# The first recurrence of a two-layer AdaLN stack in a new order: state update inside the next chunk, mix ahead of the last levels, operands and norm on ScalarE, leaf blocks as tiles

## Chip, cores and metric

One core of one Trainium2 chip. The metric is the device time of one execution in microseconds (us), the median of the runs. In the profile the engines are PE (TensorE matmul), PEld (its weight loads), DVE (VectorE), ACT (ScalarE), POOL (GpSimd) and SP (which issues DMAs).

## What is computed

Two layers, each of a recurrence and a mixture of experts, on x of 2 batches x 1024 tokens x 128 channels. The change is in the recurrence of layer 0, which the reference writes as a scan over the tokens of each batch and head (2 heads of 64):

```
x_last = jnp.pad(x, ((0, 0), (1, 0), (0, 0)))[:, :t]
dxa = x_last - x
xm = x + dxa * miu_x
lora_h = jnp.tanh(xm @ A_lora).reshape(b, t, 5, -1)
miu = lambda_ + jnp.einsum('btfi,fic->fbtc', lora_h, B_lora)
w_in, k_in, v_in, r_in, g_in = x[None] + dxa[None] * miu
k = k_in @ Wk.T; v = v_in @ Wv.T; r = r_in @ Wr.T
g = jax.nn.silu(g_in @ Wg.T)
w = td_miu + jnp.tanh(w_in @ td_A) @ td_B
def step(S, inp):            # decay = exp(-exp(w))
    ri, ki, vi, di = inp
    kv = ki[:, None] * vi[None, :]
    y = ri @ (S + uh[:, None] * kv)
    S = di[:, None] * S + kv
    return (S, y)
```

After it come a norm of y per head, the product with g, the projection Wo, the gated addition to x, and the norm that feeds the experts of layer 0.

## The kernel before

The program is four blocks of instructions, one after the other: a setup, the recurrence of layer 0 (`rwkv_phase`, the only one that changes), the experts of layer 0, and layer 1. Within a block each engine has a queue written out by hand; an engine runs its queue strictly in order, and semaphores (`s_...`) tie the queues together. No scheduler reorders anything.

The recurrence goes over the sequence in 8 chunks of 128 tokens, both batches at once (N = 256 columns). `steps` calls `front` and then `step(i, q, prepare, tail)` for chunks 0 to 7: all have `prepare` but the last, all have `tail` but the first. What one step holds:

- **Levels** (`for m in lv`, 7 of them): the decays are multiplied up in a tree. On each level DVE writes `tot` (L595) and half of `rl` (L596), ACT copies the other half of `rl` and half of `kl` (L765, L767), POOL writes the rest of `kl` (L686). Each level waits for the one below on the other engines. PE takes scores of 32x32 leaf blocks from levels 0 to 4 (`leaf_scores`, L855) and wider ones from levels 5 and 6 (L913, L919); level 7 gives the operands for the state.
- **Attention and state**: DVE masks the leaf scores (`prod`, L613), adds up five partial blocks (`leafs`, L616) and copies them into the diagonal of `att` (L621); ACT copies the blocks off the diagonal (L784 to L786). PE transposes `kl[7]` (L929), ACT copies it to `ktm` (L776), PE computes the output y (L938, L941) and k^T v (L946), DVE masks that and updates `state` (L626, L630).
- **prepare, for chunk i+1**: DVE normalises x (L504), PE transposes it (L799), ACT modulates it (L713), POOL takes the difference to the token before (L641), DVE forms `xm` (L510), PE, ACT and PE do the low-rank product (L804, L805, L718, L720, L814, L817), DVE and POOL mix five inputs (L518, L646), PE projects them (`project`, L822 to L838), ACT takes them out (L728 to L742).
- **tail, of chunk i-1**: statistics of y on DVE (L535, L539), their deviation on POOL (`deviation`, L655, L657), `yn` (L544), a transpose, the gate and Wo, the addition to x, and `moe_input`, the norm for the experts (L558 to L572, its deviation on POOL at L673, L675).

`keep_busy(n)` (L868) is n matmuls on constants whose result nobody reads. A step with a tail has 5 of them at its start and 2 x 2 further on. What lets an engine into step i is `start`:

```
if not isinstance(i, int) or i:
    eng.wait_ge(s_state, i * 3)
eng.wait_ge(s_gT, i + 1)
```

So every engine begins a step when the state of the chunk before has been written (L630) and the last projection has been taken out by ACT (L742).

## Time and profile before

| | |
|---|---|
| median of 3 runs | 767.53 us (767.01 to 770.05) |
| the profiled execution's own time | 770.7 us |
| its span in the profile | 768.6 us |
| mean granted clock of TensorE | 0.931 of full speed |
| busy: PE, DVE, ACT, POOL | 664.5, 432.5, 290.5, 277.2 us |
| recurrence of layer 0 in the span | from 23 to about 202.5 us |

A row of the timeline gives the start (us from the span's start), the duration (us; for "x4" from the first start to the last end), the engine, the line, the operation with output<-input, and in brackets how long the engine sat idle before it and who released it. A matmul of the program in float32 shows as two instructions ("x32" for 16 matmuls). "PEclk" and the figure after the PEld column in a row of windows are the clock that TensorE was granted, as a share of 2.4 GHz: 1.00 is 2.4 GHz and 0.50 is 1.2 GHz.

### The profile page before, as it was taken

Reading aid. Unit: us, or ns where it says so; the run is one execution under the profiler, and the core shown is the slowest. Engines: PE = TensorE matmul, PEld = TensorE weight load, DVE = VectorE, ACT = ScalarE, POOL = GpSimd, SP = SyncE. Lnnn points to the kernel's source line nnn. Section 1 sums busy time; section 2 is a strip of 40 time slices with the busy share of each in tenths; the row PEclk is TensorE's granted clock in tenths of the full one; section 3 lists DMA queues with packets and bytes.
Section 4 is the critical chain, followed back from the end, with each engine's and each line's share of the span. In section 5 each row is a group of like instructions: output and inputs, shape, how many; then the busy total and the mean of one; then the engine's idle time right before and its main releaser. Section 6 shows DMA issues by size and latency. Waiting matters only on the chain.

```text
span 768.6 us, 26385 instructions
## 1 busy us (share of the span) xinstructions
PE 664.5 (86%) x10885; PEld 558.9 (73%) x10885; DVE 432.5 (56%) x1364; ACT 290.5 (38%) x964; POOL 277.2 (36%) x418
## 2 busy tenths in 40 slices
PE   4688888889721979699999999999999799999996
PEld 4356666657611968478888888888887599898996
DVE  4357888886250322265867776776767455344443
ACT  0154444442110422145555454454544235333321
POOL 1235555553234456100324233342423243222216
PEclk9769999989955989599999999999999899999999
DMA  6691000000214573200000000000040247575553
GB/s 176 215 275 27 3 1 3 3 2 2 110 42 152 165 236 119 58 3 4 3 10 12 11 11 14 11 11 14 7 144 10 80 149 253 182 246 197 186 211 90
DMA packets 45910, 66.31 MB, mean 86 GB/s; under 512 B 5584, under 2 KB 34736, under 8 KB 42848
## 3 DMA queue, kind: packets, MB, share of 16 engines
q1 hardware_dynamic: 42368, 57.55, 24.1%
q0 software_dynamic: 3424, 7.08, 2.6%
q8 instruction: 87, 1.43, 0.7%
q14 instruction: 31, 0.25, 0.1%
HBM read 49.92 MB, written 19.02 MB: 90 GB/s over the span
## 4 chain that ended last, share of the span: by engine, by line
PE 53%; DVE 2%; DMA 1%; issue 1%; another core or an unknown queue 1%; ACT 0%; SPq 0%; POOL 0%; DVEq 0%; POOLq 0%
PE bank L1720 6%; PE quad L1578 5%; PE quad L1702 5%; PE quad L1704 5%; PE bank L1603 4%; PE pair L1540 3%; PE bank L1627 3%; PE bank L1640 2%; PE quad L1584 2%; PE pair L1542 2%; PE pair L1541 2%; PE bank L1643 2%; PE bank L1630 2%; PE pair L1565 2%; DMA f_xg<-moe_slots 1%
## 5 line engine op out<-in xcount | busy, mean ns | idle before, releaser
L1978 DVE TENSOR_TENSOR h_masked<-quad,const 128x1536 f32<-128x1536 f32 (+2 forms) x66 | 112.5, 1704 | 55.1 <-PE quad L1584 45.5
L1814 ACT ACTIVATE f_sa<-quad 128x256 f32<-128x256 f32 (+1 forms) x115 | 40.2, 352 | 94.9 <-PE quad L1704 77.1
L2092 DVE TENSOR_TENSOR f_hid<-f_sa,quad 128x256 f32<-128x256 f32 (+1 forms) x115 | 43.0, 380 | 55.2 <-ACT f_sa L1814 54.8
L1702 PE MATMUL quad<-f_xT,f_w 128*128 128x256 f32 (+1 forms) x190 | 51.4, 353 | 3.6 <-DVE f_hid L2092 3.6
L1720 PE MATMUL bank<-f_w,f_hid 128*128 128x128 f32 x390 | 50.7, 277 | 1.1 <-DVE f_hid L2095 0.9
L1720 PEld LDWEIGHTS bank<-f_w,f_hid 128*128 128x128 f32 x390 | 47.8, 192 | 3.6 <-DVE f_hid L2095 2.8
L1704 PE MATMUL quad<-f_xT,f_w 128*128 128x256 f32 (+1 forms) x190 | 50.2, 346 | 0.0
L2201 POOL DMA_INDIRECT moe_slots<-g_pay,g_slot x28 | 28.7, 1023 | 58.3 <-DVE g_pay L1946 43.2
L1578 PE MATMUL quad<-h_qk 32*128 32x128 f32 x1024 | 47.1, 298 | 0.0
L868 PE MATMUL bank<-const 128*128 128x256 f32 x140 | 37.3, 406 | 7.8 <-PEq L202 7.8
L1603 PE MATMUL bank<-h_qk,h_state 32*32 32x128 f32 x1024 | 42.5, 274 | 0.0
L1578 PEld LDWEIGHTS quad<-h_qk 32*128 32x128 f32 x1024 | 34.8, 187 | 10.3 <-issue 8.4
L1791 ACT ACTIVATE h_gT<-bank 128x128 f32<-128x128 f32 x64 | 17.8, 278 | 64.9 <-PE bank L1630 64.9
L1103 POOL DMA_INDIRECT moe_out<-e_yg,e_token x32 | 30.9, 965 | 28.5 <-DVE e_yg L1203 22.2
L2167 POOL TENSOR_TENSOR h_added<-h_added,mod_row 128x128 f32<-128x128 f32 x16 | 7.3, 455 | 93.8 <-ACT h_added L1787 93.8
L2269 POOL DMA_INDIRECT moe_out<-f_y,f_token x31 | 30.3, 977 | 28.9 <-DVE f_y L2104 20.4
L686 POOL TENSOR_TENSOR kl<-kl,tot 128x128 f32<-128x128 f32 x56 | 25.2, 449 | 40.6 <-DVE state L630 20.8
L1765 ACT ACTIVATE h_qk<-pair 128x256 f32<-128x256 f32 x64 | 24.5, 383 | 36.8 <-PE pair L1542 36.8
L1702 PEld LDWEIGHTS quad<-f_xT,f_w 128*128 128x128 f32 x190 | 32.3, 195 | 6.7 <-DVE f_hid L2092 3.9
L1704 PEld LDWEIGHTS quad<-f_xT,f_w 128*128 128x128 f32 x190 | 34.2, 195 | 3.4
L868 PEld LDWEIGHTS bank<-const 128*128 128x128 f32 x140 | 26.6, 203 | 11.4 <-issue 8.0
L1795 ACT ACTIVATE h_oT<-bank 128x128 f32<-128x128 f32 x64 | 17.8, 278 | 40.7 <-PE bank L1652 32.2
(380 smaller groups left out, 1840.0 us busy)
## 6 DMA issues: line engine op xcount, KB each, us to landing
f_w<-moe_w SPq DMA_DIRECT2D x23, 1088.0 KB, 5.2
e_w<-in_experts_dram SPq DMA_DIRECT2D x32, 257.5 KB
moe_slots<-blank SPq DMA_DIRECT2D x2, 2112.0 KB, 16.6
moe_slots<-zero SPq DMA_DIRECT2D x4, 516.0 KB, 4.0
e_xg<-moe_slots SPq DMA_DIRECT2D x8, 258.0 KB
f_xg<-moe_slots SPq DMA_DIRECT2D x12, 132.0 KB, 4.5
moe_w<-in_moe_w_dram SPq DMA_DIRECT2D x1, 1408.0 KB, 7.5
moe_w<-in_moe_w_dram SPq DMA_DIRECT2D x1, 1280.0 KB, 10.5
```

The costliest lines, as they stand in the source:

```text
L868: pe.matmul(bank[of][:, 0:N], cst("ident"), const[:, 0:N], start=True, stop=True)
L1103: pool.indirect_dma_start(out=t["moe0_out"], out_offset=bass.IndirectOffsetOnAxis(ap=token_of[s][:, k:k + 1], axis=0), in_=yg[s][:, k, :], ...
L1578: last = pe.matmul(quad[:, h, a * P:(a + 1) * P], qk[q][head(h), 1 - a, :], qk[q][head(h), a, :], start=True, stop=True, tile_position=(h ...
L1603: pe.matmul(left[head(h), part * P:(part + 1) * P], states[k][head(h), (0 if part else 2 * D):(D if part else 3 * D)], qk[k][head(h), 1 - ...
L1702: pe.matmul(up_bank(n, f)[:, 0:s], w[:, F1 + TAIL1 + f * P:F1 + TAIL1 + (f + 1) * P], x_of(n)[:, 0:s], start=True, stop=True)
L1704: pe.matmul(up_bank(n, f)[:, T1:T1 + s], w[:, f * P:(f + 1) * P], x_of(n)[:, 0:s], start=True, stop=True).then_inc(f_up, 1)
L1720: pe.matmul(acc[k], hid[n % 2][:, f, cols], w[:, 2 * F1 + f * C:2 * F1 + (f + 1) * C], start=(f == 0), stop=False)
L1814: act.activation(sa[g % 3][:, 0:s], up_bank(n, f)[:, 0:s], ACT.Silu).then_inc(f_sa, 1)
L1978: dve.tensor_tensor(masked[k % 4][:, :, a * P:z * P], quad[:, :, a * P:z * P], cst("causal")[:, None, a * P:z * P].to_broadcast([P, HPG, ( ...
L2092: dve.tensor_tensor(hid[n % 2][:, f, 0:s], sa[g % 3][:, 0:s], up_bank(n, f)[:, T1:T1 + s], ALU.mult)\
L2201: pool.indirect_dma_start(out=t["moe1_slots"], out_offset=bass.IndirectOffsetOnAxis(ap=slot[:, b * 2 + k:b * 2 + k + 1], axis=0), in_=pay[ ...
L2269: pool.indirect_dma_start(out=t["moe1_out"], out_offset=bass.IndirectOffsetOnAxis(ap=token_of[n % 2][:, k:k + 1], axis=0), in_=yg[n % 2][: ...
```

## The change

- `start` no longer waits for the state but for the last score matmul of the chunk before (`s_leafmm`). The state update is now `carry`, on DVE in the next step behind its level 2, behind the norm's statistics.
- Masked leaf scores are no longer reduced and copied into `att`. One addition folds five partial blocks into three (`s_sum`), and PE multiplies each 32x32 block with `v` by itself, as a tile on the array's diagonal: 24 small matmuls for each batch.
- `rd` and `kd` (operands of the leaf scores with the bonus) and the centring of x come from ACT instead of DVE. ACT's bias column `nbias` is made once. `rd`, `kd` and `gT` are doubled.
- DVE's `mix` moves from behind the last level to behind level 4, POOL's to behind level 5. `gate` moves to the step's start, `normalise` behind `mix`, `output` to the step's end. The norm for the experts is split and runs two chunks behind instead of one.
- On PE, `lora` comes one level earlier, `mix` ahead of level 4's scores, the projections ahead of the scores of levels 5 and 6, the transpose of x(i+2) at the end of step i. The transposes of `kl[7]` and the product with `ktm` stand behind the output matmuls. ACT copies `ktm` as the last thing of a step. Of 9 `keep_busy` matmuls in a middle step 2 are left.

The diff, cut to its core:

```diff
-            if not isinstance(i, int) or i:
-                eng.wait_ge(s_state, i * 3)
+            if i:
+                eng.wait_ge(s_leafmm, i)
             eng.wait_ge(s_gT, i + 1)
...
+            def carry(n, q):
+
+                dve.tensor_tensor(kv[:, :, :], bank[5][:, N:2 * N].rearrange("p (b n) -> p b n", b=BATCH),
+                                  cst("head2")[:, None, :].to_broadcast([P, BATCH, P]), ALU.mult).then_inc(s_state, 1)
+                dve.wait_ge(s_state, n * 3 + 1)
+                for b in range(BATCH):
+                    dve.scalar_tensor_tensor(out=state[:, b, :], in0=state[:, b, :], scalar=tots[q][LEVELS][:, b:b + 1],
+                                             in1=kv[:, b, :], op0=ALU.mult, op1=ALU.add).then_inc(s_state, 1)
...
-                    norm(i + 1)
-                if tail:
-                    statistics(i - 1, 1 - q)
-
-                rh, kh = halves(rl[0], 0), halves(kl[0], 0)
-                dve.tensor_scalar(halves(rd, 0)[:, :, 0], rh[:, :, 0], bonus[:, 0:1], None, ALU.mult).then_inc(s_diag, 1)
-                dve.tensor_copy(halves(rd, 0)[:, :, 1], rh[:, :, 1]).then_inc(s_diag, 1)
-                dve.tensor_copy(halves(kd, 0)[:, :, 0], kh[:, :, 0]).then_inc(s_diag, 1)
-                dve.tensor_scalar(halves(kd, 0)[:, :, 1], kh[:, :, 1], bonus[:, 0:1], None, ALU.mult).then_inc(s_diag, 1)
+                    last_column(i + 1)
+                gate(i, q)
...
+                    if i and m == LEVELS - 1:
+                        dve.wait_ge(s_kv, i)
...
-                    if tail and m == 0:
-                        normalise(i - 1, 1 - q)
                     if prepare and m == 1:
                         lora_input(i + 1)
+                    if m == 2:
+                        if i >= 2:
+                            moe_statistics(i - 2)
+                        if tail:
+                            statistics(i - 1, 1 - q)
+                            carry(i - 1, 1 - q)
                     if m == 4:
+                        if prepare:
+                            mix(i + 1)
+                        if i >= 2:
+                            moe_scale(i - 2)
                         if tail:
-                            dve.wait_ge(s_zg, i)
-                        gate(i)
-                        if tail:
-                            output(i - 1, 1 - q)
-                if prepare:
-                    mix(i + 1)
+                            normalise(i - 1, 1 - q)
...
-                                  ALU.add).then_inc(s_leaf, 1)
-                dve.wait_ge(s_leaf, i + 1)
-                for k in range(4):
-                    rows = slice(k * LEAF, (k + 1) * LEAF)
-                    dve.tensor_copy(att[rows, :, rows], leafs[rows, :, :]).then_inc(s_att, 1)
+                dve.tensor_tensor(prod[:, :, 0:2 * LEAF], prod[:, :, 0:2 * LEAF], prod[:, :, 2 * LEAF:4 * LEAF],
+                                  ALU.add).then_inc(s_sum, 1)
                 if tail:
...
-                    if prepare and m == 1:
+                    if prepare and m == 0:
                         difference(i + 1)
-                    if tail and m == 0:
-                        deviation(i - 1, 1 - q)
-                    if tail and m == 2:
-                        gated_heads(i - 1, 1 - q)
+                    if m == 2:
+                        if i >= 2:
+                            moe_deviation(i - 2, q)
+                        if tail:
+                            deviation(i - 1, 1 - q)
+                    if prepare and m == 5:
+                        mix(i + 1)
                 if tail:
+                    gated_heads(i - 1, 1 - q)
...

+            def centre(n):
+                for b in range(BATCH):
+                    c = n + b * CHUNKS
+                    act.activation(xn[:, b, :], x_bc[:, b, n, :], ACT.Identity, bias=nbias[:, c:c + 1],
+                                   scale=rstd[:, c:c + 1]).then_inc(s_xn, 1)
...
+                kd, k0 = halves(kds[q], 0), bank[2][:, 0:N].rearrange("p (k h e) -> p k h e", h=2, e=1)
+                act.activation(kd[:, :, 0], k0[:, :, 0], ACT.Copy).then_inc(s_evac, 1)
+                act.activation(kd[:, :, 1], k0[:, :, 1], ACT.Copy, scale=bonus[:, 0:1]).then_inc(s_evac, 1)
...
+                rd, r0 = halves(rds[q], 0), bank[3][:, 0:N].rearrange("p (k h e) -> p k h e", h=2, e=1)
+                act.activation(rd[:, :, 0], r0[:, :, 0], ACT.Copy, scale=bonus[:, 0:1]).then_inc(s_diag, 1)
+                act.activation(rd[:, :, 1], r0[:, :, 1], ACT.Copy).then_inc(s_diag, 1)
...
                                    ACT.Copy).then_inc(s_rc, 1)
                     if prepare and m == 0:
                         modulate(i + 1)
-                    if tail and m == 1:
-                        scale_heads(i - 1, 1 - q)
-                    if prepare and m == 3:
+                    if prepare and m == 2:
                         lora_tanh(i + 1)
-                act.wait_ge(s_ktT, i + 1)
-                act.activation(ktm[:, :, :], bank[4][:, 0:N].rearrange("p (b n) -> p b n", b=BATCH),
-                               ACT.Copy).then_inc(s_ktm, 1)
+                    if m == 3 and i + 2 < CHUNKS:
+                        centre(i + 2)
+                    if m == 5:
+                        if i:
+                            act.wait_ge(s_kv, i)
+                        if prepare:
+                            decay_tanh(i + 1)
+                            take_k_v(i + 1, 1 - q)
+                        if tail:
+                            scale_heads(i - 1, 1 - q)
                 if prepare:
-                    decay_tanh(i + 1)
-                    take_k_v(i + 1, 1 - q)
+                    take_decay_r_g(i + 1, 1 - q)
...
-                    take_decay_r_g(i + 1, 1 - q)
+                    act.wait_ge(s_ktT, i + 1)
+                    act.activation(ktm[:, :, :], bank[4][:, 0:N].rearrange("p (b n) -> p b n", b=BATCH),
+                                   ACT.Copy).then_inc(s_ktm, 1)
...
-                keep_busy(5 if tail else 2)
+                keep_busy(2)
...
-                    if tail and m == 1:
-                        keep_busy(2)
-                        transpose_heads(i - 1, 1 - q)
-                    if prepare and m == 2:
-                        lora(i + 1)
-                    elif m == 2:
-                        keep_busy(3, 2)
-                    if tail and m == 3:
-                        output(i - 1, 1 - q)
+                    if m == 1:
+                        if prepare:
+                            lora(i + 1)
+                        else:
+                            keep_busy(3, 2)
+                    if m == 3:
+                        if prepare:
+                            mix(i + 1)
+                        else:
+                            keep_busy(3, 2)
                 if prepare:
-                    mix(i + 1)
+                    project_k_v(i + 1)
+                if tail:
+                    transpose_heads(i - 1, 1 - q)
+                if prepare:
+                    project_decay_r_g(i + 1)
+                else:
+                    keep_busy(5, 2)
...
                 pe.wait_ge(s_r, i * LEVELS + 7)
                 pe.wait_ge(s_rc, i * 2 * LEVELS + 14)
-                if tail:
-                    pe.wait_ge(s_gated, i)
-                for b in range(BATCH):
-                    last = pe.transpose(bank[4][:, b * P:(b + 1) * P], kl[7][:, b * P:(b + 1) * P], cst("ident"))
-                last.then_inc(s_ktT, 1)
-                if prepare:
-                    project(i + 1)
-                else:
-                    keep_busy(5, 2)
-                pe.wait_ge(s_att, i * 4 + 4)
-                pe.wait_ge(s_off, i * 3 + 3)
+                if i:
+                    pe.wait_ge(s_state, i * 3)
+                pe.wait_ge(s_sum, i + 1)
                 for b in range(BATCH):
                     pe.matmul(bank[5][:, b * P:(b + 1) * P], rl[7][:, b * P:(b + 1) * P], state[:, b, :],
                               start=True, stop=False, skip_group_check=True)
+                    for l in (0, 1, 4):
+                        for h in range(RW_HEADS):
+                            for k in range(4):
+                                rows = slice(k * LEAF, (k + 1) * LEAF)
+                                pe.matmul(bank[5][rows, b * P + h * RW_DIM:b * P + (h + 1) * RW_DIM],
+                                          prod[rows, h * BATCH + b, l * LEAF:(l + 1) * LEAF],
+                                          v_sb[rows, b, h * RW_DIM:(h + 1) * RW_DIM], start=False, stop=False,
+                                          tile_position=(k * LEAF, k * LEAF), skip_group_check=True)
+                    if b == 0:
+                        pe.wait_ge(s_off, i * 3 + 3)
                     for h in range(RW_HEADS):
-                        pe.matmul(bank[5][:, b * P + h * RW_DIM:b * P + (h + 1) * RW_DIM], att[:, h * BATCH + b, :],
-                                  v_sb[:, b, h * RW_DIM:(h + 1) * RW_DIM], start=False, stop=True,
-                                  skip_group_check=True)
-                pe.wait_ge(s_ktm, i + 1)
-                for b in range(BATCH):
-                    last = pe.matmul(bank[5][:, N + b * P:N + (b + 1) * P], ktm[:, b, :], v_sb[:, b, :], start=True,
-                                     stop=True, skip_group_check=True)
+                        last = pe.matmul(bank[5][:, b * P + h * RW_DIM:b * P + (h + 1) * RW_DIM],
+                                         att[:, h * BATCH + b, :], v_sb[:, b, h * RW_DIM:(h + 1) * RW_DIM],
+                                         start=False, stop=True, skip_group_check=True)
+                if prepare:
+                    pe.wait_ge(s_k, i * LEVELS + 7)
+                    if tail:
+                        pe.wait_ge(s_gated, i)
+                    for b in range(BATCH):
+                        last = pe.transpose(bank[4][:, b * P:(b + 1) * P], kl[7][:, b * P:(b + 1) * P], cst("ident"))
+                    last.then_inc(s_ktT, 1)
+                    pe.wait_ge(s_ktm, i + 1)
+                    for b in range(BATCH):
+                        last = pe.matmul(bank[5][:, N + b * P:N + (b + 1) * P], ktm[:, b, :], v_sb[:, b, :], start=True,
+                                         stop=True, skip_group_check=True)
```

**ACT, end of a middle step.** Names: `ktm` the transposed keys, `tw` to `eg` the projections of the next chunk, `att` the score blocks, `rl<-rl_1` the first level of the next step. Before:

```order
L767 ACTIVATE kl<-kl 128x2x64
L776 ACTIVATE ktm<-bank 128x256
L724 ACTIVATE tw<-quad 64x256
L728 ACTIVATE kl_1<-quad 128x256
L729 ACTIVATE v_sb<-quad 128x256
L784 ACTIVATE att<-pair 64x4x64
L785 ACTIVATE att<-pair 32x4x32
L786 ACTIVATE att<-pair 32x4x32
L735 ACTIVATE ew<-quad,td_miu 128x256
L737 ACTIVATE tot_1<-ew 128x256
L742 ACTIVATE eg<-quad 128x256
L765 ACTIVATE rl<-rl_1 128x128
```

After the change:

```order
L782 ACTIVATE zT<-bank,beta,gamma 128x256
L796 ACTIVATE rl<-rl 128x2x64
L798 ACTIVATE kl<-kl 128x2x64
L758 ACTIVATE ew<-quad,td_miu 128x256
L760 ACTIVATE tot_1<-ew 128x256
L765 ACTIVATE rd<-quad,bonus 128x128
L766 ACTIVATE rd<-quad 128x128
L768 ACTIVATE eg<-quad 128x256
L819 ACTIVATE att<-pair 64x4x64
L821 ACTIVATE att<-pair 32x4x32
L824 ACTIVATE ktm<-bank 128x256
L796 ACTIVATE rl<-rl_1 128x128
```

The copy of `ktm` moved from the head of this stretch to its very end, right ahead of the next step's first level.

**PE, from the last leaf scores of a middle step to the next step.** Names: `lh` and `xx` the low-rank and mixed inputs, `pair` the scores, `bank<-const` both the transposes (128x128) and `keep_busy` (128x256). Before:

```order
L855 MATMUL pair<-rl,kl 32x32 x16
L814 MATMUL quad<-lh,b_pad 128x256 x4
L817 MATMUL quad<-lh,b_last 128x256
L913 MATMUL pair<-rl,kl 32x32 x8
L919 MATMUL pair<-rl,kl 64x64 x4
L929 MATMUL bank<-const,kl 128x128 x2
L822 MATMUL quad<-xx,td_a 64x256
L838 MATMUL quad<-xx,wT 128x256
L938 MATMUL bank<-state,rl 128x128
L941 MATMUL bank<-v_sb,att 128x64 x2
L946 MATMUL bank<-v_sb,ktm 128x128 x2
L868 MATMUL bank<-const 128x256 x5
```

After the change:

```order
L879 MATMUL quad<-xx,wT 128x256
L959 MATMUL pair<-rl,kl 32x32 x8
L965 MATMUL pair<-rl,kl 64x64 x4
L916 MATMUL bank<-wT,zT 128x128 x2
L838 MATMUL quad<-const,xn 128x128 x2
L979 MATMUL bank<-state,rl 128x128
L985 MATMUL bank<-v_sb,prod 32x64 x24
L992 MATMUL bank<-v_sb,att 128x64 x2
L985 MATMUL bank<-v_sb,prod 32x64 x24
L1000 MATMUL bank<-const,kl 128x128 x2
L1004 MATMUL bank<-v_sb,ktm 128x128 x2
L911 MATMUL bank<-const 128x256 x2
```

The transposes of `kl` moved from ahead of the projections to behind all output matmuls; 48 block matmuls joined them there.

**DVE, the middle of a step after the change.** Names: `xm` the input of the low-rank product, `nst` and `h_pay` the norm for the experts, `gst` and `gmv` the norm of y.

```order
L509 SCALAR_TENSOR_TENSOR xm<-dxa,miu,hT 128x256
L601 TENSOR_TENSOR tot<-tot 128x32
L602 TENSOR_TENSOR rl<-rl,tot 128x32x4
L567 BN_STATS nst<-x_sb 128x6 x2
L571 BN_AGGR nmv<-nst 128x2 x2
L574 SCALAR_TENSOR_TENSOR h_pay<-x_sb,nmv,sbw 128x128 x2
L535 BN_STATS gst<-bank 128x6 x4
L539 BN_AGGR gmv<-gst 128x2 x4
L556 TENSOR_TENSOR kv<-bank,const 128x256
L560 SCALAR_TENSOR_TENSOR state<-state,tot,kv 128x128 x2
L601 TENSOR_TENSOR tot<-tot 128x16
L602 TENSOR_TENSOR rl<-rl,tot 128x16x8
```

Six groups of the tail that stood at a step's end or start now stand between levels 2 and 3.

## Rows read from the trace of the kernel before

**Rows 1.** The page: the granted clock in 40 slices of the span.

```profile
PEclk9769999989955989599999999999999899999999
```

**Rows 2.** Windows: PE, PEld, DVE, ACT, POOL busy, clock, DMA share, GB/s.

```profile
98.00:117.00 19.00, 16.04 (x257) 11.23 (x256) 15.97 (x60) 9.20 (x31) 10.96 (x20) 1.00 0.00 1
```

**Rows 3.** State updates (one tile) in four windows: durations in ns, first and last start.

```profile
L630 DVE SCALAR_TENSOR_TENSOR state<-state,tot,kv x2: 347/350/352, 96.9 to 97.1; 128x128 f32<-128x128 f32 x2
...
L630 DVE SCALAR_TENSOR_TENSOR state<-state,tot,kv x2: 347/350/352, 115.6 to 115.9; 128x128 f32<-128x128 f32 x2
...
L630 DVE SCALAR_TENSOR_TENSOR state<-state,tot,kv x2: 345/348/352, 153.7 to 154.0; 128x128 f32<-128x128 f32 x2
L630 DVE SCALAR_TENSOR_TENSOR state<-state,tot,kv x2: 347/350/353, 175.1 to 175.3; 128x128 f32<-128x128 f32 x2
```

**Rows 4.** Timeline of DVE, one step (chunk 3).

```profile
98.34 0.61 DVE L535 BATCH_NORM_STATS2 gst<-bank 128x6 f32<-128x64 f32 x4
99.05 0.38 DVE L539 BATCH_NORM_AGGREGATE gmv<-gst 128x2 f32<-128x6 f32 x4
...
102.75 0.67 DVE L510 SCALAR_TENSOR_TENSOR xm<-dxa,miu,hT 128x256 f32<-128x256 f32 x1
...
109.37 0.81 DVE L613 TENSOR_TENSOR prod<-pair,const 128x640 f32<-128x640 f32 x1
...
112.50 0.49 DVE L558 BATCH_NORM_STATS2 nst<-x_sb 128x6 f32<-128x128 f32 x2
...
113.38 0.62 DVE L565 SCALAR_TENSOR_TENSOR h_pay<-x_sb,nmv,sbw 128x128 f32<-128x128 f32 x2
```

**Rows 5.** Timeline of POOL, the same step.

```profile
100.19 1.17 POOL L657 TENSOR_TENSOR grs<-grs,eps_pow 128x4 f32<-128x4 f32 x1
...
101.76 0.61 POOL L641 TENSOR_TENSOR dxa<-hT 128x256 f32<-128x256 f32 x1
...
104.36 1.09 POOL L686 TENSOR_TENSOR kl<-kl,tot 128x128 f32<-128x128 f32 x2
...
108.03 3.01 POOL L646 TENSOR_TENSOR xx<-xx,hT 128x256 f32<-128x256 f32 x5
```

**Rows 6.** Timeline of ACT, the same step.

```profile
99.01 0.81 ACT L713 ACTIVATE hT<-quad,mod_col 128x128 f32<-128x128 f32 x2 [0.97 <-PE quad L799]
...
108.11 0.39 ACT L776 ACTIVATE ktm<-bank 128x256 f32<-128x256 f32 x1 [0.77 <-PE bank L929]
```

**Rows 7.** Timeline of PE, the same step.

```profile
106.99 0.33 PE L913 MATMUL pair<-rl,kl 64*32 64x32 f32 x16
107.25 0.45 PE L919 MATMUL pair<-rl,kl 64*64 64x64 f32 x8
107.63 0.44 PE L929 MATMUL bank<-const,kl 128*128 128x128 f32 x2
...
109.90 0.70 PE L826 MATMUL quad<-xx,wT 128*128 128x256 f32 x2 [0.54 <-POOL xx L646]
...
112.59 0.46 PE L938 MATMUL bank<-state,rl 128*128 128x128 f32 x2
...
113.95 0.66 PE L946 MATMUL bank<-v_sb,ktm 128*128 128x128 f32 x4
```

**Rows 8.** Timeline of PE, layer 1: tiles of 32x32 on the diagonal (L1603).

```profile
343.38 0.31 PE L1603 MATMUL bank<-h_qk,h_state 32*32 32x128 f32 x4
...
343.51 0.29 PE L1603 MATMUL bank<-h_qk,h_state 32*32 32x128 f32 x4
```

**Rows 9.** Windows, PE alone: PE busy, clock, in the step of chunk 6.

```profile
166.00:167.00 1.00, 0.46 (x2) 1.00 0.05 16
167.00:168.00 1.00, 1.00 (x5) 0.55 0.00 0
```

**Rows 10.** Timeline, the stage's edges: ACT's first level of chunk 0, DVE's last norm.

```profile
40.06 0.32 ACT L765 ACTIVATE rl<-rl 128x128 f32<-128x128 f32 x1
...
201.88 0.61 DVE L572 SCALAR_TENSOR_TENSOR h_pay<-h_pay,nrstd,sbw 128x128 f32<-128x128 f32 x2 [0.66 <-POOL nrstd L675]
```

More of the change, by code:

```diff
@@ L519, in mix, with gate @@
                                              op0=ALU.add, op1=ALU.mult).then_inc(s_scaled, 1)
-            def gate(n):
-                dve.scalar_tensor_tensor(out=gT[:, :], in0=eg[:, :], scalar=1.0, in1=bank[0][:, N:2 * N], op0=ALU.add,
+            def gate(n, q):
+                dve.scalar_tensor_tensor(out=gTs[q][:, :], in0=eg[:, :], scalar=1.0, in1=bank[0][:, N:2 * N], op0=ALU.add,
                                          op1=ALU.mult).then_inc(s_gate, 1)
             def front():
-                norm(0)
+                last_column(0)
                 lora_input(0)
@@ L615, in step, with last_norms @@
                 dve.wait_ge(s_prod, i + 1)
[L616 to L633 removed]
+                dve.tensor_tensor(prod[:, :, 0:2 * LEAF], prod[:, :, 0:2 * LEAF], prod[:, :, 2 * LEAF:4 * LEAF],
+                                  ALU.add).then_inc(s_sum, 1)
+                if tail:
+                    output(i - 1, 1 - q)
+            def last_norms(n, q):
+                moe_statistics(n - 1)
+                normalise(n, q)
+                moe_scale(n - 1)
+                output(n, q)
+                moe_statistics(n)
+                moe_scale(n)
+            steps(dve, front, step, (statistics, last_norms))
         @block.gpsimd
@@ L922, in step @@
                 last.then_inc(s_leafmm, 1)
-                pe.wait_ge(s_k, i * LEVELS + 7)
+                if tail:
+                    output(i - 1, 1 - q)
+                if i + 2 < CHUNKS:
+                    transpose_x(i + 2)
                 pe.wait_ge(s_r, i * LEVELS + 7)
                 pe.wait_ge(s_rc, i * 2 * LEVELS + 14)
-                if tail:
-                    pe.wait_ge(s_gated, i)
-                for b in range(BATCH):
-                    last = pe.transpose(bank[4][:, b * P:(b + 1) * P], kl[7][:, b * P:(b + 1) * P], cst("ident"))
-                last.then_inc(s_ktT, 1)
-                if prepare:
-                    project(i + 1)
-                else:
-                    keep_busy(5, 2)
-                pe.wait_ge(s_att, i * 4 + 4)
-                pe.wait_ge(s_off, i * 3 + 3)
+                if i:
+                    pe.wait_ge(s_state, i * 3)
+                pe.wait_ge(s_sum, i + 1)
                 for b in range(BATCH):
```

81 lines of the change are left out of this document (43 added, 38 removed).

## The prediction

> **What bounds the kernel now.** I read the granted clock on the page first [rows 1], then the windows by stage, then the state updates, then the timeline of each engine in one step. The recurrence fills 23 to 202.5 us of a span of 768.6, and nothing else changes. A middle step takes 18.8 us from state to state (96.9 to 115.6 [rows 3]). In 19 us DVE is busy 15.97, the most of any engine but PE, whose 16.04 hold nine `keep_busy` matmuls [rows 2]. The reader should see in DVE's timeline an engine that hardly rests and does one thing after another that all others wait for: levels, mix, leaf sums, expert norm, state [rows 4]. So DVE's queue is the bound, and the state at its end is what all engines' `start` waits for.
>
> The second thing to see is the clock. In the step of chunk 6 PE worked 0.46 of a microsecond and then was granted 0.55, that is the fall from 2.4 to 1.2 GHz [rows 9]. Ahead of that fall PE had only small tiles and waited for POOL's mix. That step took 21.4 us from state to state (153.7 to 175.1) where its neighbours take 18.8 [rows 3]: one low stretch costs **2.6 us**.
>
> **What the change takes from DVE.** Per step it removes the sum and the copies of the leaf blocks (the time between the mask's end at 110.18 and 112.50, 2.3 us [rows 4]), the centring of x and four operand copies (an estimate of 1.4 from the two-to-four-instruction groups beside them), and adds one fold of 256 columns. I put the fold at 0.4, an estimate between the 0.67 of `xm` with its 256 columns and half the 0.81 of the mask with 640 [rows 4]. Net about 3.3 us less DVE work in a step. If DVE stayed the bound, that would be the gain.
>
> **But the queue of ACT closes a new loop.** ACT now copies `ktm` as a step's last thing, and its first level of the next step stands right behind. The copy waits for PE's transposes of `kl[7]`, which wait behind all output matmuls, which wait for the fold of the leaf scores. I follow this loop for a middle step at 2.4 GHz, from ACT's first level at 0:
>
> 1. ACT: two level copies (0.45, an estimate from the 0.32 of one [rows 10]), then the modulation, 0.81 [rows 6]: 1.3. It cannot run earlier, though DVE and POOL have their halves done.
> 2. POOL's difference 0.61 [rows 5]: 1.9. DVE's `xm` 0.6 [rows 4]: 2.5. DVE's level 2, 0.3: 2.8.
> 3. DVE: first part of the expert norm, 112.50 to 114.00 in the rows of before, 1.5: 4.3. Statistics of y, 98.34 to 99.43, 1.1 [rows 4]: 5.4. `carry` follows on DVE (1.1), off this path.
> 4. POOL: deviation, from the statistics at 99.43 to 101.36 [rows 4, 5], 1.9: 7.3. In its queue the levels 3, 4 and 5 stand behind it: 1.09 for two [rows 5], so 1.4 up to its mix: 8.7. DVE's mix is ready by then (levels 3 and 4 done at about 7.1, first output 0.4 later) and so is PE's low-rank part (about 6).
> 5. POOL's mix: three of five, 3.01 x 3/5 = 1.8 [rows 5]: 10.5, and 0.1 to PE.
> 6. PE: from the first projection at 109.90 to the output matmuls at 112.59, 2.7 [rows 7], plus the transpose of the heads that now stands in between, 0.3: 13.6. Scores of levels 5 and 6, 106.99 to 107.70, 0.7 [rows 7]: 14.3.
> 7. DVE: mask 0.86, fold 0.4 [rows 4]: 15.6. PE's product with Wo and its transpose of x fit in here, as do ACT's `rd`, `eg` and `att` copies: ACT is free of them at about 16.3.
> 8. PE: output matmuls 1.36 (112.59 to 113.95 [rows 7]) plus the 48 blocks. They are 96 instructions. Tiles of 64x32 with 32 columns came every 16 ns (16 from 106.99 to 107.25 [rows 7]); tiles of 32x32 on the diagonal with 128 columns every 32 ns (four from 343.38 to 343.51 [rows 8]). The blocks have 64 columns; I take 16 ns, 1.5 us, because they hold half the columns of the diagonal tiles, and keep 0 (hidden by overlap) and 32 ns (3.1) as ends: 18.5.
> 9. Transposes of `kl` 0.44 [rows 7], ACT's `ktm` 0.39 [rows 6]: **19.3**.
>
> So the loop is 0.5 us longer than DVE's 18.8. What DVE gives up turns into waiting.
>
> The Trainium skill, "TensorEngine Tiling (Array Packing)", section "Key Properties", says that a change of tiling mode drains TensorE. This would add to item 8, where a step now changes mode four times more; at the 0.27 that I estimate for one matmul's passage it would make the sum 1.1 larger per step, 20.4. No row here separates such a drain.
>
> **The edges.** Chunk 0 has neither item 3 nor the heads: about 16.8. Chunk 1 has no expert norm yet: 17.8. Chunks 2 to 6 take 19.3 each, 96.5. The last chunk and what follows it: levels 2, norms, levels and fold to 11.5, output 14.4, statistics, two expert norms and the drain to about 25.0, against the 26.8 up to 202.5 [rows 10], since the sum and the copies are gone. Together 156.1 against 162.4 [rows 10]: **-6.3 us** at full clock.
>
> **The clock.** Before, PE waited 0.54 us ahead of its second projection [rows 7] and had `keep_busy` in the longer gaps. Now seven of nine are gone, and by the items above PE has only small tiles and a 32-row mix from 3.9 to 5.9, then 0.4 us of tiles, a half-microsecond matmul near 9.4, and starts its projections at 10.6. That is emptier than the stretch ahead of the fall in chunk 6 [rows 9], and it comes in every step with `prepare`. After the fall come the projections, scores and heads (item 6), which are now on the loop. I charge the 2.6 of rows 3, a little less since part of the low stretch lies under waits: 2.5 for each of seven steps, +17.5. Ends: 0 if the clock holds, and 3.4 a step (all of items 6, at twice the time).
>
> The Trainium skill, "TensorE: Matmul & The Clock Gate", section "What's actually happening", has the same rule against this change: "the default state is throttled, and activity releases the throttle". By that rule the sum has this term, without it it is 761; the trace agrees as far as the fall of rows 9 goes.
>
> **Sum.** -6.3 + 17.5 = +11.2. The profiled execution took 770.7 in all (768.6 span and 2.1 around), so it would be 781.9; it stands 3.2 over the median of the runs, which gives 778.7 there. I forecast **778 us**.
>
> **Rivals.**
> - *The clock holds.* The leaf tiles and 48 new blocks count as enough work. For it: before, the clock stood through PE's waits for POOL, such as 0.54 us [rows 7], in all middle steps but one [rows 1]. Against it: the step where it didn't. Then only the -6.3 is left: **761 us, faster**. It decides from fewer than about two and a half low stretches (6.3 / 2.5).
> - *DVE remains the bound.* ACT's wait for `ktm` is covered, because DVE and POOL start earlier than I think and the modulation is not what they wait for. Then a step is 18.8 - 3.3 = 15.5, seven of them -23: **745 us**. Against it is ACT's queue, where `ktm` stands ahead of the first level with nothing between.
> - *The clock falls in half of the steps*, or for half as long: +8.75 - 6.3: **770 us**.
> - *The blocks are slow*, 32 ns an instruction, or drain the array: +1.5 in seven steps, 10.5 more: **789 us**.
>
> **How the numbers follow.** About 0.5% (3.8 us) is what a measurement of this kernel can tell from no change, so the middle band is 763.7 to 771.4. Forecast (771 to 787 by itself) 0.45, of it 0.43 slower and 0.02 in the band. Clock holds 0.25, of it 0.20 faster and 0.05 in the band. DVE bound 0.09, faster. Half 0.11: 0.01, 0.07, 0.03. Slow blocks 0.10, slower. Sums: faster 0.30, same 0.14, slower 0.56. The range runs from 757 to 790: left out are the DVE rival, the top half of the slow blocks and the lowest part of the held clock, 0.18 together. It takes in the unknown price of the blocks and of the fold.
>
> **What would show it.** Right: granted clock of 0.50 in a part of each step; DVE idle before level 1, waiting for ACT; ACT idle before `ktm`, waiting for PE; POOL's levels 3 waiting for DVE's statistics; steps of 21 to 22 us, or 19.3 where the clock holds. The blocks should take 0.8 us per batch. Wrong: a clock of 1.00 throughout, or steps under 18 us with ACT's first level hard behind `eg`. Then the tail of PE, or the gap before the projections, is shorter than I made it.

## The result, and the profile after

| | before | after |
|---|---|---|
| median of runs (range) | 768.76 us (767.01 to 770.05, 4 runs) | **793.79 us** (790.75 to 796.16, 4 runs) |
| profiled execution / span | 770.7 / 768.6 us | 790.75 / 789.0 us |
| mean granted clock | 0.931 | 0.902 |
| recurrence, ACT's first level to DVE's last norm, us from the span's start | 40.06 to 202.5 | 40.3 to 224.4 |

The change makes the kernel slower: ratio 1.0325, 95% interval 1.0273 to 1.0377. Forecast were 778 us, in a range of 757 to 790; the sign is right, the size is not. Here and below a median is that of all runs of a set, while a ratio and its interval compare the fast runs of both kernels alone.

All of it is in the recurrence: it grew by 21.6 us, from 162.4 to 184.1, and the rest of the profiled execution took 1.6 less. The page of the kernel after: part 1, the line of the granted clock in 40 slices (19.7 us each), and from part 5 the row of DVE's level product:

```profile
PE 675.9 (86%) x11555; PEld 566.1 (72%) x11555; DVE 410.7 (52%) x1282; ACT 300.4 (38%) x1011; POOL 276.0 (35%) x418
...
PEclk9687886895895598879999999999999999999999
...
L601 DVE TENSOR_TENSOR tot<-tot 128x128 f32<-128x128 f32 (+6 forms) x56 | 17.0, 303 | 32.2 <-ACT kl L798 30.5
```

Two things are to be seen. The clock, in slices 3 to 11, was near 1.00 before but for single dips [rows 1]; now nearly every slice of the stage is below. And DVE idles 32.2 us ahead of the level line `tot`, 30.5 of it for ACT's level, where DVE's wait for that was 4.8 us before: the engine that was the bound now waits for ACT's level.

One step from ACT's first level to the next, with the part of it at 1.2 GHz in brackets, of chunk 0 to 6, then the last to the end of the stage:

```
before  19.8 (11.0) 18.8 (0)    18.9 (0)   18.8 (0)    18.8 (0)    19.2 (0)   21.4 (6.8)  26.8
after   18.8 (4.2)  22.3 (10.2) 21.6 (6.8) 25.8 (16.0) 22.2 (11.3) 21.0 (3.4) 25.8 (16.7) 26.6 (3.7)
```

17.8 us of the stage were at 1.2 GHz before, 72.4 after. The loop that the forecast followed stands in the timeline of the step of chunk 3, each engine by itself (start and duration in us, then idle time before it and who ended it). ACT:

```profile
128.50 0.38 ACT L824 ACTIVATE ktm<-bank 128x256 f32<-128x256 f32 x1 [6.47 <-PE bank L1000]
128.78 0.31 ACT L796 ACTIVATE rl<-rl 128x128 f32<-128x128 f32 x1
```

DVE:

```profile
120.34 0.82 DVE L622 TENSOR_TENSOR prod<-pair,const 128x640 f32<-128x640 f32 x1 [5.21 <-PE pair L965]
...
129.42 0.23 DVE L601 TENSOR_TENSOR tot<-tot 128x64 f32<-128x64 f32 x1 [5.98 <-ACT kl L798]
...
130.71 0.67 DVE L509 SCALAR_TENSOR_TENSOR xm<-dxa,miu,hT 128x256 f32<-128x256 f32 x1 [0.86 <-POOL dxa L646]
```

POOL:

```profile
130.06 0.61 POOL L646 TENSOR_TENSOR dxa<-hT 128x256 f32<-128x256 f32 x1 [6.77 <-ACT hT L733]
```

ACT idles 6.47 us for PE's transposes of `kl`, copies `ktm`, and only then takes the level. DVE and POOL stand still for six microseconds each behind that. PE in the same step:

```profile
110.61 0.39 PE L898 MATMUL pair<-rl,kl 64*32 64x32 f32 x32 [1.71 <-POOL kl L693]
112.32 0.72 PE L861 MATMUL quad<-xx,td_a 128*64 128x256 f32 x2 [1.32 <-POOL xx L651]
113.66 1.22 PE L865 MATMUL quad<-xx,wT 128*128 128x256 f32 x2 [0.62 <-POOL xx L651]
...
122.47 1.50 PE L985 MATMUL bank<-v_sb,prod 32*32 32x64 f32 x48
```

Windows of the same step (us; PE, PEld, DVE, ACT, POOL busy; granted clock; DMA share; GB/s):

```profile
111.00:112.00 1.00, 0.00 (x1) 0.00 (x0) 1.00 (x4) 0.61 (x3) 0.79 (x3) 1.00 0.00 0
112.00:113.00 1.00, 0.68 (x2) 0.19 (x2) 1.00 (x3) 0.00 (x0) 1.00 (x3) 0.88 0.00 0
113.00:114.00 1.00, 0.38 (x2) 0.35 (x2) 1.00 (x5) 0.38 (x1) 1.00 (x2) 0.50 0.00 0
114.00:124.00 10.00, 10.00 (x95) 7.15 (x94) 4.10 (x12) 4.69 (x16) 3.36 (x6) 0.50 0.01 2
124.00:133.00 9.00, 8.53 (x133) 6.75 (x134) 2.58 (x11) 2.41 (x9) 1.65 (x4) 0.50 0.01 2
133.00:134.00 1.00, 1.00 (x4) 0.33 (x3) 0.90 (x7) 0.00 (x0) 0.85 (x2) 0.88 0.00 0
```

PE stands almost still at 111, as the forecast had it, and the clock falls from 1.00 to 0.50 within the next two. What was not in the forecast: it stays at 0.50 for 20.5 us (112.8 to 133.2) although PE was busy for 10.00 of 10.00 from 114 on. The projections, scores, output matmuls and transposes, all of the loop's PE part, ran at half speed.

### The profile page after: what moved, and what is told of

It is laid out like the page before. It is cut to its first block, busy times and chain, and to the rows that moved or that the text cites. A ratio compares the mean times of both kernels' runs of the same rounds, so it can differ in the third digit from the quotient of the medians.

```text
span 789.0 us, 27723 instructions
## 1 busy us (share of the span) xinstructions
PE 675.9 (86%) x11555; PEld 566.1 (72%) x11555; DVE 410.7 (52%) x1282; ACT 300.4 (38%) x1011; POOL 276.0 (35%) x418
## 4 chain that ended last, share of the span: by engine, by line
PE 51%; DVE 2%; DMA 1%; issue 1%; another core or an unknown queue 1%; ACT 0%; POOL 0%; SPq 0%; DVEq 0%; POOLq 0%
PE bank L1778 6%; PE quad L1636 5%; PE quad L1760 5%; PE quad L1762 4%; PE bank L1661 4%; PE pair L1598 3%; PE bank L1685 3%; PE bank L1698 2%; PE quad L1642 2%; PE pair L1599 2%; PE pair L1600 2%; PE bank L1688 2%; PE bank L1701 2%; PE pair L1623 2%; DMA f_xg<-moe_slots 1%
## 5 line engine op out<-in xcount | busy, mean ns | idle before, releaser
L1849 ACT ACTIVATE h_gT<-bank 128x128 f32<-128x128 f32 x64 | 17.8, 278 | 64.3 <-PE bank L1688 64.3
L1853 ACT ACTIVATE h_oT<-bank 128x128 f32<-128x128 f32 x64 | 17.8, 278 | 42.4 <-PE bank L1710 32.9
L601 DVE TENSOR_TENSOR tot<-tot 128x128 f32<-128x128 f32 (+6 forms) x56 | 17.0, 303 | 32.2 <-ACT kl L798 30.5
L1598 PE MATMUL pair<-h_hT,hla_wq 128*128 128x128 f32 x128 | 30.7, 323 | 2.5 <-POOL h_hT L2219 1.8
```

The source lines that it names most:

```text
L1598: pe.matmul(proj[:, 0:P], W["q"][:, cols], hT[b][:, :], start=True, stop=True)
```

## The experiments

Three questions are open after this. How much is the clock, how much the order? Is it the loop through `ktm`? And what do the 32x32 blocks cost? Ratios are to the kernel before, which ran with each set: median 767.19 us beside e1 to e4, 765.04 beside e5 to e8. A filler (`keep_busy(1)`) is one matmul, in two instructions of 0.26 us each. The stage is counted from ACT's first level to DVE's last norm in the profiled execution; what comes behind it took 561 to 570 us in these executions, so steps and stages are compared first. The columns on the stage and its steps are each from one profiled execution.

| | median us | ratio to before | stage us | of it at 1.2 GHz | later steps us |
|---|---|---|---|---|---|
| before | 767.19 / 765.04 | | 162.4 | 17.8 | 18.8 |
| after | 793.79 | 1.0325 | 184.1 | 72.4 | 21.0 to 25.8 |
| e1_fill | 775.17 | 1.0122 | 168.1 | 6.8 | 19.9 |
| e2_before_two | 801.51 | 1.0458 | 192.1 | 119.5 | 23.9 |
| e3_early | 758.78 | 0.9883 | 155.0 | 33.5 | 16.9 to 17.2 |
| e4_early_fill | 760.89 | 0.9941 | 154.0 | 0.6 | 18.2 |
| e5_start9 | 797.20 | 1.0413 | 187.4 | 44.4 | 21.1 or 23.3 |
| e6_fill_oneblock | 766.05 | 0.9987 | 159.8 | 7.3 | 19.0 |
| e7_early_light | 753.39 | 0.9837 | 145.1 | 0.6 | 16.9 to 17.1 |
| e8_early_re | 750.24 | 0.9820 | 146.1 | 10.6 | 16.8 to 17.0 |

### e1_fill: filler matmuls in the two gaps

```diff
                         if prepare:
                             mix(i + 1)
+                            keep_busy(4)
 ...
                 if prepare:
+                    keep_busy(3)
                     project_k_v(i + 1)
```

> The changed kernel with seven of the removed constant matmuls put back, but at places where PE waits for POOL: four ahead of level 4's scores and three behind them, in every step that prepares. Nothing else moves. Theory (the clock): the stretches at 1.2 GHz in the recurrence shrink from 72 us to under 15, and of the 28 us that they cost by the changed kernel's trace at least 20 come back: 765 to 773 us. Rival 1 (the clock is granted low for another reason, such as the small tiles): low time unchanged, 792 to 798. Rival 2 (the loop through ACT is itself much longer than 19.3 us a step): clock at 1.00 and still 778 or more.

Measured: 775.17 us (768.41 to 779.47), ratio 1.0122 (1.0077 to 1.0167). 6.8 us at 1.2 GHz instead of 72.4; the page's clock line reads

```profile
PEclk9789999999855889799999999999999899999999
```

The steps are 22.7, 19.4, and then 19.9 five times, all at full clock from the second on. So the clock is more than half of the loss (1.0325 to 1.0122), and even without it a middle step is 1.1 us longer than before. The low time came out as the theory had it; the time is 2 us above its range, since 18.6 us came back where it asked for 20. Rival 2's 778 is not reached, but a part of what it says is there: a middle step is 0.6 longer than the 19.3 forecast. The fillers themselves cost in the first two steps: in chunk 1 k's projection begins 10.15 us after the first level, in the kernel after 9.15. In the middle steps they cost nothing, and there the loop can be checked item by item. The step of chunk 3 begins with ACT's level at 99.81. POOL:

```profile
108.45 3.28 POOL L651 TENSOR_TENSOR xx<-xx,hT 128x256 f32<-128x256 f32 x5
```

PE:

```profile
110.47 0.70 PE L865 MATMUL quad<-xx,wT 128*128 128x256 f32 x2 [0.43 <-POOL xx L651]
...
114.09 0.71 PE L916 MATMUL bank<-wT,zT 128*128 128x128 f32 x4
...
115.63 0.46 PE L981 MATMUL bank<-state,rl 128*128 128x128 f32 x2 [0.62 <-DVE prod L625]
116.02 0.87 PE L987 MATMUL bank<-v_sb,prod 32*32 32x64 f32 x48
116.83 0.66 PE L994 MATMUL bank<-v_sb,att 128*128 128x64 f32 x4
117.32 0.44 PE L981 MATMUL bank<-state,rl 128*128 128x128 f32 x2
...
118.99 0.39 PE L1002 MATMUL bank<-const,kl 128*128 128x128 f32 x2
```

ACT:

```profile
119.41 0.38 ACT L824 ACTIVATE ktm<-bank 128x256 f32<-128x256 f32 x1 [3.37 <-PE bank L1002]
119.69 0.31 ACT L796 ACTIVATE rl<-rl 128x128 f32<-128x128 f32 x1
```

| loop item, us after ACT's first level | forecast | e1_fill |
|---|---|---|
| POOL's mix begins | 8.7 | 8.64 |
| k's projection begins | 10.6 | 10.66 |
| scores end (the next matmul begins) | 14.3 | 14.28 |
| output matmuls begin, after mask and fold | 15.6 | 15.82 |
| transposes of `kl` begin | 18.5 | 19.18 |
| ACT's next first level | 19.3 | 19.88 |

The chain was traced rightly through four engines to within 0.2 us; the largest part of the rest is the output matmuls, 3.36 us (115.63 to 118.99) instead of 2.86. The fillers did not hold this step back: k's projection still waited 0.43 for POOL.

### e3_early: `ktm` before the output matmuls

This undoes one part of the change, the place of the transposes, and leaves its clock alone. They go to another PSUM bank, since the old one is in use there.

```diff
                 last.then_inc(s_leafmm, 1)
+                if prepare:
+                    pe.wait_ge(s_k, i * LEVELS + 7)
+                    pe.wait_ge(s_rc, i * 2 * LEVELS + 14)
+                    for b in range(BATCH):
+                        last = pe.transpose(bank[2][:, b * P:(b + 1) * P], kl[7][:, b * P:(b + 1) * P],
+                                            cst("ident"))
+                    last.then_inc(s_ktT, 1)
                 if tail:
                     output(i - 1, 1 - q)
 ...
-                    for b in range(BATCH):
-                        last = pe.transpose(bank[4][:, b * P:(b + 1) * P], kl[7][:, b * P:(b + 1) * P], cst("ident"))
-                    last.then_inc(s_ktT, 1)
```

and ACT's copy of `ktm` goes ahead of its three `att` copies.

> The changed kernel with the transposes of kl[7] right behind the last score matmuls (into the free half of another PSUM bank) and ACT's copy of them ahead of its att copies, so that ACT no longer waits for the output matmuls before the next step's first level. No constant matmuls added. Theory (the loop closes through ACT's ktm): about 2.7 us a step at full clock and up to 6 where the clock is low, 7 steps: 766 to 776. Rival (DVE or PE is right behind, or the clock falls for longer since the gaps stay): 783 to 792.

Measured: **758.78 us** (752.72 to 777.61), ratio 0.9883 (0.9836 to 0.9929), better than expected. The ten runs spread wide, with mean granted clocks from 0.936 down to 0.895 (e1's and e4's lowest is 0.934), so this median is the least steady of the table. In the profiled execution, a step at full clock takes 16.9 to 17.2 us instead of 19.9, and the time at 1.2 GHz is 33.5 us. The releaser of the waits shows that the loop is gone. PE and ACT of e3, chunk 6, each from its own timeline:

```profile
164.29 0.44 PE L973 MATMUL quad<-const,kl 128*128 128x128 f32 x2
...
165.84 0.46 PE L986 MATMUL bank<-state,rl 128*128 128x128 f32 x2 [0.66 <-DVE prod L625]
```

```profile
164.77 0.38 ACT L819 ACTIVATE ktm<-quad 128x256 f32<-128x256 f32 x1
...
165.82 0.27 ACT L825 ACTIVATE att<-pair 32x128 f32<-32x128 f32 x1
```

The copy waits for nothing, and ACT is free at 166.09 while PE is only beginning its output matmuls. They now lie beside the next step's levels. The place of two pieces of work, the transposes and ACT's copy, decides the sign of the whole change.

### e4_early_fill: both

> Both edits together: early ktm and the seven constant matmuls in PE's gaps. Theory (clock and loop are separate terms): 747 to 757, faster than both kernels. Rival (the fillers now delay PE, which starts the next step late because output matmuls and k^T v run into it): 760 to 770.

Measured: 760.89 us (758.0 to 766.09), ratio 0.9941 (0.9901 to 0.9981). The two do not add: the rival's range held, not the theory's. The clock is almost clean (0.6 us low), but the steps are 18.2 instead of 17.1. PE of e4, just before k's projection:

```profile
158.16 1.56 PE L911 MATMUL bank<-const 128*128 128x256 f32 x6
159.66 0.65 PE L861 MATMUL quad<-xx,td_a 128*64 128x256 f32 x2
160.23 0.70 PE L865 MATMUL quad<-xx,wT 128*128 128x256 f32 x2
```

Neither projection has a wait ahead of it; in e3 the first waits 1.00 and k's 0.55 for POOL. The fillers are in front, and PE is late by them. A filler is free only inside a gap, and with `ktm` early the gap is shorter than seven of them.

### e2_before_two: the kernel before with two fillers a step

The other side of the same question: if fillers matter this much, how much do the seven that the change drops matter to the old order?

```diff
-                keep_busy(5 if tail else 2)
+                keep_busy(2)
                 start(pe, i)
 ...
-                if tail:
-                    keep_busy(2)
 ...
                     if tail and m == 1:
-                        keep_busy(2)
                         transpose_heads(i - 1, 1 - q)
```

> The kernel before with the constant matmuls of a middle step cut from nine to two, nothing else changed. Theory (the clock): low stretches appear in most steps; at 2.6 us for one of 6.8 us that is 5 to 13 us more, 773 to 781. Rival (in the kernel before PE is not on the path that ends a step, since DVE is busy throughout, so a low clock is mostly hidden): within 3 us of before, 766 to 771.

Measured: 801.51 us (799.47 to 801.62), ratio 1.0458 (1.0383 to 1.0534), much more than either theory said. Every step from chunk 1 to 6 has 17.1 us at 1.2 GHz and takes 23.9 instead of 18.8. DVE of this kernel in one step, two of the waits that it did not have before:

```profile
142.74 2.05 DVE L518 SCALAR_TENSOR_TENSOR xx<-quad,lamb,dxa 128x256 f32<-128x256 f32 x5 [1.19 <-PE quad L817]
...
153.18 0.42 DVE L626 TENSOR_TENSOR kv<-bank,const 128x256 f32<-128x256 f32 x1 [2.58 <-PE bank L943]
```

At half speed PE takes DVE's place as the bound. Seven dummy matmuls, 3.6 us of PE's time a step, are worth 34 us (801.51 - 767.19) to the kernel.

### e5_start9: nine fillers, all at the step's start

```diff
-                keep_busy(2)
+                keep_busy(9 if tail else 2)
                 start(pe, i)
```

> The changed kernel with the same seven constant matmuls put back, but all at the step's start, where PE has work anyway, instead of in its waits for POOL. Theory (what counts is the empty stretch between the low-rank part and the projections): the clock still falls in most steps, low time in the recurrence stays above 35 us, 785 us or more, and the start is delayed by 1.5 us a step. Rival (the sum of work per step is what counts): low time as in the kernel with fillers in the gaps, 775 to 780.

Measured: 797.2 us (794.66 to 806.94), ratio 1.0413 (1.035 to 1.0476). A middle step has as many fillers as in e1, and the time is no better than with two. Of the 44.4 us at 1.2 GHz 20.5 lie in chunk 0, which has no more fillers here than in the kernel after (its low time was 4.2 us there, in another execution). In chunks 1 to 6, which have nine, it is 23.8 us, against 64.4 with two and 0 in e1. So the number helps the clock too, but only the gaps ahead of the projections kept it up throughout. And at the start they cost time: a step at full clock takes 21.1 us instead of 19.9, since the leaf tiles and PE's low-rank product stand behind them (L843 begins 5.4 us after ACT's first level, in e1 2.7).

### e6_fill_oneblock: what the blocks cost

e1 with 16 instead of 48 block matmuls in a step, 64 instructions fewer; part of the attention within 32 tokens is left out.

```diff
-                    for l in (0, 1, 4):
+                    for l in (0,):
```

> The kernel with seven fillers in the gaps, and of the three blocks per head and row group only the first multiplied with v: 16 block matmuls instead of 48, so part of the attention within 32 tokens is left out of the output. Theory (the blocks stand on the loop at 17 ns an instruction): 64 instructions fewer, 1.1 us a step, steps of 18.8 instead of 19.9 at full clock, 8 us less in all. Rival (hidden behind ACT's copies): no change. Rival 2 (less work brings the clock down): low stretches come back.

Measured: 766.05 us (760.21 to 768.41), ratio 0.9987 (0.9945 to 1.0029). The steps take 19.0 instead of 19.9: 0.9 us for 64 instructions, 14 ns each. PE's output matmuls in chunk 3 of e6:

```profile
114.69 0.46 PE L981 MATMUL bank<-state,rl 128*128 128x128 f32 x2 [0.61 <-DVE prod L625]
115.08 0.43 PE L987 MATMUL bank<-v_sb,prod 32*32 32x64 f32 x16
...
117.15 0.39 PE L1002 MATMUL bank<-const,kl 128*128 128x128 f32 x2
```

They take 2.46 us (114.69 to 117.15) where e1's take 3.36: the same 0.9. So the blocks are on the loop at full price (nothing hides them), and that price is near the 16 ns taken; the slow-blocks rival is out. All 96 are 1.3 us of a step by these 14 ns.

### e7_early_light and e8_early_re: the version that beats both

e7 is e3 with two fillers behind the mix (`keep_busy(2)` after `mix(i + 1)`); e8 has three there and none at the start, and moves the expert norm out of the way of the statistics of y:

```diff
                     if m == 2:
-                        if i >= 2:
-                            moe_statistics(i - 2)
                         if tail:
                             statistics(i - 1, 1 - q)
-                            carry(i - 1, 1 - q)
+                        if i >= 2:
+                            moe_statistics(i - 2)
                     if m == 4:
                         if prepare:
                             mix(i + 1)
-                        if i >= 2:
-                            moe_scale(i - 2)
                         if tail:
+                            carry(i - 1, 1 - q)
                             normalise(i - 1, 1 - q)
+                if i >= 2:
+                    moe_scale(i - 2)
```

and on POOL `moe_deviation` goes behind the last level.

> Early ktm with only two constant matmuls added, between the mix and level 4's scores. Theory: they fit in PE's wait for POOL, so a step keeps the 17.1 us that the early version shows at full clock, and the low time in the recurrence falls from 33 us to below 14: 7 to 10 us less than the early version, 748 to 753. Rival (two are too few): as the early version, 755 to 760.

> Early ktm, three constant matmuls after the mix and none at the step's start; DVE takes the statistics of y ahead of the expert norm's first part and the state update behind its mix, and the expert norm's deviation moves behind POOL's last level. Theory: the deviation of y is out of POOL's way 1.4 us earlier, PE reaches its low-rank part 0.5 us earlier, so a middle step takes 16.2 to 16.7: 742 to 748. Rival (PE's low-rank part is right behind and sets the mix): 16.8 to 17.1 a step, 748 to 753.

Measured: e7 753.39 us (750.84 to 754.56), ratio 0.9837 (0.9792 to 0.9881), 17.1 a step and 0.6 us low: as the theory had it, at the upper end of its range. Two fillers in the first of PE's gaps were enough in its profiled execution. e8 **750.24 us** (749.37 to 755.08), ratio 0.982 (0.9769 to 0.9871), 16.7 to 17.0 a step and 10.6 low, all of it in chunk 0: its theory (16.2 to 16.7 a step, 742 to 748 us) missed, its rival's figures came out. Between the two the intervals overlap, and the stage of e8 is no shorter than e7's; that its reordering gained is shown only by the middle step, 0.1 to 0.3 us. The gain on before is settled for both: 16 to 17 us of the stage. One step of e8 in the windows:

```profile
107.50:124.40 16.90, 15.07 (x342) 10.82 (x341) 14.70 (x50) 10.65 (x37) 10.63 (x20) 1.00 0.01 3
```

DVE is busy 14.70 of 16.90, so DVE is near to being the bound again, as the rival "DVE remains the bound" wanted, though not at its 15.5 us; most of the change's saving on DVE then shows as time.

## Why the prediction was wrong in size and right in sign

**DVE's load fell as said, and became waiting.** DVE's busy time on the page went from 432.5 to 410.7 us, 2.7 for each of eight chunks, where 3.3 was said. The waits in the profile after and e3 show that at full clock the saving was lost to the loop.

**The loop through `ktm` was real.** e1 confirms items 1 to 7 to 0.2 us, and e3, which moves the transposes and their copy and nothing else of the computation, takes 2.8 us off each step at full clock.

**Item 8 was mis-sized: it put the changes between whole array and tiles at nothing.** It had 2.86 for the output matmuls, 1.36 of them for those of before and 1.5 for the blocks; they took 3.36. Over the 1.36 they took 2.00 more with 96 block instructions (e1) and 1.10 more with 32 (e6). That is 14 ns an instruction, 1.34 for all 96 and a little under the 1.5 put, and 0.65 that does not grow with the number of blocks. The row of the blocks in e1 agrees with the 14: 0.87 us for 48, less the 0.21 of a single one, are 0.66 for 47 distances. The 0.65 stands over the four changes between whole array and tiles in a step, 0.16 each, if each costs the same. Part of it can be seen in the starts. PE of the kernel before, behind the 112.59 of [rows 7]:

```profile
112.88 0.56 PE L941 MATMUL bank<-v_sb,att 128*128 128x64 f32 x4
113.28 0.44 PE L938 MATMUL bank<-state,rl 128*128 128x128 f32 x2
```

From the state product to what follows it were 0.29 us there (112.59 to 112.88), and 0.39 in e1 where blocks follow; `att` took 0.40 up to the next product, and 0.49 in e1 where blocks stand ahead. The Trainium skill, "TensorEngine Tiling (Array Packing)", section "Key Properties", has a rule that a change of tiling mode drains TensorE. A fixed price at each change agrees with it in sign, though no run separates a drain from other causes, such as the first weight loads; the prediction's estimate beside its sum, 1.1 a step, was 1.7 times the 0.65.

**The edges were a little short as well.** Chunk 0: 18.8 less the price of its 4.2 us at 1.2 GHz (0.30 for each, see below), an estimated 17.5 where 16.8 was put. Chunk 1: e1's 19.4 less the 1.0 by which its fillers delayed k's projection, 18.4 where 17.8 was put. The last chunk takes 26.6 (e1, all at full clock), 25.0 was put. Of the 5.9 us in all some 4 are the half microsecond of output matmuls, eight times. The stage at full clock comes to 17.5 + 18.4 + 5 x 19.9 + 26.6 = 162.0 us, not 156.1: the gain of 6.3 is nearly gone, **0.4** in its place. With the clock held the changed kernel would take about 769 in the profiled execution (790.75 - 22.1), where before took 770.7: hardly any gain, so the rival "the clock holds, 761" would have missed too.

**The clock term was right in kind and low in size.** 184.1 - 162.0 = 22.1 us against 17.5. What failed in this term is the length of a low stretch: it was charged at the price of the 6.8 us of chunk 6 in each of seven steps, 48 us in all, and there were 72.4, above all because two stretches went on for 20.5 us through the output matmuls into the next step. The price per low microsecond was on the high side: 2.6 / 6.8 = 0.38 from the step of chunk 6 [rows 3]; here it is 22.1 / 72.4, about 0.30, in e2 5.1 / 17.1 = 0.30, and between e3 and e7, which differ by two fillers, 127.1 - 117.2 = 9.9 us in the first seven steps for 32.9 less low, 0.30. That it is well under one half fits with part of a low stretch lying under waits. The rule of the Trainium skill, "TensorE: Matmul & The Clock Gate", section "What's actually happening", that activity releases the throttle, has the sign; e5 and e1 show that the place of the activity counts too: with nine fillers at the start of chunks 1 to 6 these were low for 23.8 us, with two there and seven in the gaps for none.

**Which step failed.** Two terms of the sum were too small, and the first weighs more: the full-clock part, put at -6.3 and measured at -0.4, above all because item 8 (and with it the edges) had nothing for the changes between whole array and tiles; and the clock, put at +17.5 and measured at +22.1, because the low stretches were taken as shorter than they were.

**Sum in the profiled execution:** +5.9 for the full-clock part, +4.6 for the clock, -1.6 outside the stage: 8.9, and 781.9 + 8.9 = 790.8, where 790.75 was measured. The median lies 3.0 above that (the other runs had a clock of 0.892 to 0.898 against 0.902); the forecast had also taken 3.2 off for a profiled run of before that lay above its median.

**The range** ended at 790 because the slow end was made of one mishap, slow blocks. Two ordinary errors on the slow side (output matmuls, length of the low stretches) and the 3.0 between the profiled execution and the median went past it together. That the sign came out is not luck: the loop and the falling clock, from which it was forecast, are both in the trace.

What stays open: why some low stretches last 3.4 or 6.8 us and others 20.5 with the same instructions in the step. No run takes that apart.

## What to carry to other kernels

When work is taken off the bound, follow each in-order queue round one full step of the loop: a copy placed last on one engine, waiting for the end of another, and ahead of the first thing that everyone needs, turns the whole gain into idle time, and moving it by a few instructions gives it back. Here that was 2.8 of 19.9 us a step. Treat filler matmuls as part of the schedule: before taking them out, price the lower clock by the low stretches that the trace already shows, and put them only where PE would idle, since beyond the gap they cost time (e4's five more than e7's made its step 1.1 us longer). Count a change of PE between whole array and tiles as an instruction of its own (an estimated 0.16 us here, from e1 and e6).

## What the runs showed of the hardware that was not expected

- Seven fillers fewer a step (0.5 us each) put the kernel before at 1.2 GHz for 17.1 of 23.9 us in every step from chunk 1 to 6: 34 us, 4.6%, more than the change itself.
- A low stretch can go on for 20.5 us (112.8 to 133.2) with PE busy 10.00 of 10.00 us in it.
- Instructions on 32x32 blocks on the diagonal with 64 columns cost 14 ns each at 2.4 GHz (64 fewer took 0.9 us off the step). With the change back to the whole array counted in, 48 of them took 0.81 us at 2.4 GHz (e1) and 1.43 at 1.2 GHz (after).
- A change between whole-array matmuls and tiles cost about 0.16 us, an estimate: four of them share the 0.65 us that is left when the blocks are counted at 14 ns.
